# A four-layer graph network on one core: the four sums of a step added up in PSUM by block before DVE takes them over

## The reference, cut to what matters

```python
h = jnp.maximum(_layernorm(x, axis=-1), 0.0)     # before each layer
# layer 0: segment_sum(h[src] * weight, dst), product with W, batch norm, relu
# layer 1
messages = jax.nn.relu(x @ W_msg.T + b_msg)
aggregated = jax.ops.segment_sum(messages[src], dst, num_segments=x.shape[0])
# layer 2
msg_in = jnp.concatenate([h[src], h[dst], e], axis=-1)
messages = jax.nn.silu(msg_in @ w1 + b1) @ w2 + b2
messages = messages * jax.nn.sigmoid(msg_in @ wg + bg)
agg = segment_sum(messages, dst) / jnp.maximum(segment_sum(ones, dst), 1.0)[:, None]
# layer 3: 256 message values for each edge
mid_s0 = w0 * se * es
mid_s1 = w3 * jnp.einsum('eui,ei->eu', ve, ev) / SQRT3
mid_v0 = (w1 * se)[:, :, None] * ev[:, None, :]
mid_v1 = (w2 * es)[:, :, None] * ve
ns, nv = segment_sum(mid_scal, dst) / 4, segment_sum(mid_vec, dst) / 4
```

## Time and profile before

| | |
|---|---|
| median of three runs | 5316.91 us (5315.05 to 5318.62) |
| the profiled execution | 5316.99 us, its span 5315.3 us |
| busy: PE | 4052.6 us (76%) |
| busy: DVE | 3452.5 us (65%) |
| busy: ACT | 1883.2 us (35%) |
| busy: POOL | 3748.9 us (71%) |

### The profile page before, as it was taken

The page is one execution under the profiler, slowest core; times in us unless marked ns, Lnnn a source line. Parts: engine busy times, 40 slices in busy tenths (PEclk is TensorE's granted clock), DMA queues, the critical chain, the costliest instruction groups (busy, mean ns, idle before and its releaser), DMA issues. The chain is left out here.

```text
span 5315.3 us, 109575 instructions
## 1 busy us (share of the span) xinstructions
PE 4052.6 (76%) x21313; PEld 3103.9 (58%) x21314; DVE 3452.5 (65%) x11120; ACT 1883.2 (35%) x5384; POOL 3748.9 (71%) x3284
## 2 busy tenths in 40 slices
PE   2888888888884466666667899999998678787787
PEld 2666666666663244444445677777777555555556
DVE  6655565655553633333335788888887688888886
ACT  2322222222221122222222444333433555555553
POOL 1788888888885377777773477777776277777772
PEclk9555555555555778888788999999999888888889
DMA  5665665566666266666663566666665233233232
GB/s 171 104 90 88 93 89 93 89 93 89 93 89 119 67 180 178 181 180 179 180 179 102 159 202 198 198 196 197 195 198 159 79 57 56 56 56 57 56 56 58
DMA packets 936530, 658.88 MB, mean 124 GB/s; under 512 B 402828, under 2 KB 878955, under 8 KB 934290
## 3 DMA queue, kind: packets, MB, share of 16 engines
q0 software_dynamic: 211152, 281.46, 26.3%
q1 hardware_dynamic: 722294, 372.22, 26.2%
q10 hardware_dynamic: 2812, 2.00, 0.1%
HBM read 462.32 MB, written 224.57 MB: 129 GB/s over the span
## 5 line engine op out<-in xcount | busy, mean ns | idle before, releaser
L726 POOL DMA_INDIRECT sums<-work,idx x832 | 1288.2, 1548 | 323.4 <-issue 176.7
L1495 DVE TENSOR_TENSOR x_and_big<-psum,x_and_big 128x129 f32 (+2 forms) x2496 | 823.9, 330 | 709.7 <-PE psum L842 489.9
L758 POOL DMA_INDIRECT G<-table,src_it x832 | 861.0, 1035 | 322.9 <-issue 253.2
L758 POOL DMA_INDIRECT G<-table,work x782 | 770.5, 985 | 269.6 <-issue 236.5
L758 POOL DMA_INDIRECT x_and_big<-table,work x782 | 762.5, 975 | 273.4 <-issue 236.8
L895 PE MATMUL psum<-work 128*128 128x128 f32 x1664 | 627.5, 479 | 193.6 <-DVE work L1542 169.8
L1142 ACT ACTIVATE work<-psum,work 128x128 f32<-128x128 f32 x832 | 305.8, 368 | 1069.7 <-PE psum L887 1066.2
L895 PEld LDWEIGHTS psum<-work 128*128 128x128 f32 x1664 | 412.6, 307 | 381.4 <-DVE work L1542 378.1
L842 PE MATMUL psum<-x_and_big,oh 128*128 x1664 | 332.1, 361 | 365.1 <-DMA x_and_big<-table,work 251.7
L989 PE MATMUL psum<-x_and_big,oh 128*128 x1664 | 508.4, 459 | 130.3 <-DVE x_and_big L1682 119.7
L887 PE MATMUL psum<-x_and_big,work 128*128 x1664 | 589.5, 457 | 0.0
(11 more groups left out here) (240 smaller groups left out, 7285.8 us busy)
## 6 DMA issues: line engine op xcount, KB each, us to landing
work<-e_pre SPq DMA_DIRECT2D x832, 128.0 KB
e_pre<-work SPq DMA_DIRECT2D x196, 512.0 KB
G<-e_meta SPq DMA_DIRECT2D x832, 64.0 KB
work<-e_a SPq DMA_DIRECT2D x195, 128.0 KB
e_a<-in_edge_attr_dram SPq DMA_DIRECT2D x51, 488.0 KB
sums<-work,idx POOLq DMA_INDIRECT x832
G<-table,src_it POOLq DMA_INDIRECT x832
sums<-x_and_big POOLq DMA_DIRECT2D x4, 3264.0 KB
```

The costliest lines, as they stand in the source:

```text
L726: pool.indirect_dma_start(sums[k % COPIES], bass.IndirectOffsetOnAxis(ap=idx[:, k:k + 1], axis=0), z_out[:, k, :], None, compute_op=ALU.ad ...
L758: pool.indirect_dma_start(to, None, tab, bass.IndirectOffsetOnAxis(ap=of[:, n:n + 1], axis=0)).then_inc(quad_in[n // 4 % AHEAD], 16)
L1495: v.tensor_tensor(to, ps, to, ALU.add).then_inc(EDGE[layer]["acc_done"], 1)
```

## The change

The four products of a step now go to one window in PSUM that has four slots, one for each of four consecutive blocks from the block of the step's first item on. Items with the same block add up in the same slot. For that

- the prologue computes `slot_row`, for each item its block less that of its step's first item (0 to 3), and takes at least one item for each block, so that four consecutive items never reach over more than four blocks. `blk_row`, `row_row` and `slot_row` become partitions 0, 32 and 64 of one tensor, `item_rows`;
- PE loads 16 slot numbers beside the 16 row or block numbers every fourth step, and the place of products two to four comes from a register;
- before the four products PE sets the window to zero by products of a row of zeros with ones, both bf16: two of 128x2x129 in layer 1, one of 128x512 in layer 2, two of 128x512 in layer 3. The four products then add to what is there (`start=False`);
- DVE adds the whole window to four consecutive blocks of `acc[layer]` with one instruction (`add_window`; 128x516, 128x512 and 128x1024), at the place where the first of the four adds stood;
- `acc` has three more blocks in each layer. In layer 3 they are taken from the room of x: six more blocks of x go to `x_keep` and back (34 of 50, 28 before), and the cleared areas grow from 6450, 6400 and 12800 to 6837, 6784 and 13568 elements a partition.

```diff
-KEEP = (NBT * (D + L3W) - RING3 * L3W) // D
+KEEP = (NBT * D + (NBT - 3) * L3W - RING3 * L3W) // D
...
+            def window(win, j, reg):
+
+                return win[:, 0, :] if j == 0 else at(win, pe.snap(reg, min_val=0, max_val=3))
+
+            def zero_bank(to):
+
+                t.matmul(to, zeros_b[0:1, :], ones_b[0:1, 0:1].unsqueeze(2).broadcast_to([1, to.shape[1], to.shape[2]]), start=True, stop=True)
...
                 def top(item):
                     pe.load(regs, row_row[0:1, bass.ds(item + (LEAD - 4), RING)])
+                    pe.load(slots, slot_row[0:1, bass.ds(item + (LEAD - 4), RING)])
...
-                            pe.wait_ge(ph["acc_done"], 4 * q - 8)
+                            pe.wait_ge(ph["acc_done"], q - 2)
                         pe.wait_ge(ph["oh_ready"], q)
+                        for lo in (0, 2):
+                            t.matmul(win1[o][:, lo:lo + 2, :], zeros_b[0:1, :],
+                                     ones_b[0:1, 0:1].unsqueeze(2).broadcast_to([1, 2, wid]), start=True, stop=True)
                         for j in range(4):
                             slot = pe.snap(regs[k % 4 * 4 + j], min_val=0, max_val=ROWS - 1) % RING1
-                            mm = t.matmul(bank[2 * o + j // 2][:, j % 2 * wid:(j % 2 + 1) * wid], oh[:, (k - 1) % 4 * 4 + j, :],
-                                          at(G1, slot), start=True, stop=True)
+                            mm = t.matmul(window(win1[o], j, slots[k % 4 * 4 + j]), oh[:, (k - 1) % 4 * 4 + j, :],
+                                          at(G1, slot), start=False, stop=True, skip_group_check=True)
...
                         if item(8):
-                            pe.wait_ge(ph["acc_done"], 4 * q - 28)
+                            pe.wait_ge(ph["acc_done"], q - 7)
+                        zero_bank(win2[(k - 6) % 2])
                         pe.wait_ge(ph["msg_done"], q - 5)
...
+                        for h in (0, 2):
+                            zero_bank(win3[k % 2][:, h:h + 2, :])
...
+            link(v.tensor_scalar(D_[:, 0:NB], D_[:, 0:NB], 1.0, None, ALU.max))
...
-            def add_item(layer, reg, ps, before):
+            def add_window(layer, reg, win, landed_quads, before):
 
                 b = dve.snap(reg, min_val=0, max_val=NB)
-                to = at(acc[layer], b)
+                to = acc[layer][:, bass.ds(b, 4), :]
+                dve.wait_ge(EDGE[layer]["agg_done"], landed_quads)
                 if before is not None:
                     dve.wait_ge(EDGE[layer]["acc_done"], before)
-                v.tensor_tensor(to, ps, to, ALU.add).then_inc(EDGE[layer]["acc_done"], 1)
+                v.tensor_tensor(to, win, to, ALU.add).then_inc(EDGE[layer]["acc_done"], 1)
```

76 lines of the change are left out of this document (32 added, 44 removed).

## The result

The changed kernel takes 5335.3 us (median of five runs, 5333.2 to 5343.7) against 5316.9 (5313.1 to 5318.6) of the kernel before on the same chip: a ratio of 1.0041, 95% interval 1.003 to 1.0052. It is 18 us slower; 5309.5 was forecast, with "within 0.2%" as the likeliest case. The profiled execution, one of the longer of the five, has a span of 5341.4 us, 26.1 more than that of before. On another chip the same kernel took 5338.3 against 5310.2 (1.0044, interval 1.003 to 1.0058).

What follows compares the result with a forecast made beforehand. POOL's train of gathers, plus a draining tail, was taken to bound each layer. The terms −5.5 − 5 + 1 + 2.1 + 0 = −7.4 us gave 5309.5 against the median of 5316.91; range 5288 to 5340.

Steps and rivals of the forecast that it cites:

- Rival (b): Slower by PE in layer 2: its step becomes 5.6 us, over 5.35, costing +52 us, time 5362; chance 12%.
- Part 1: DVE's 2496 adds (823.9 us) become 624 sums (539 us): 285 us less busy time, nothing on the path.
- Part 2: PE's zeros and addresses: +0.3 to 0.9 us a step, hidden; layer 2's step 5.08, at most 5.3, under 5.35.
- Part 3: Layer 1 after its last gather: 13 PE groups at 2.0 us each, −5.5 us, between −0.3 and −12.
- Part 4: Layer 3 after its last gather: 13 steps of 2.45 us, −5 us; at half clock a loss up to 18.
- Part 5: The end of layer 2, its last three steps and final adds: +1 us, from −1 to +3.
- Part 6: What is cleared and copied: +2.1 us, of which clearings 1.3 and the prologue 0.8.
- Part 7: Gathers lengthened by DVE instructions with both operands in SBUF: 0, ±15 us; −3 in layer 2, +3 in layer 3.
- rival (c): Slower by gathers: layer 3's two-SBUF instructions catch one every step, +17 up to +35, 5327 to 5345 us; chance 13%.

Runs made afterwards that it cites:

- e_before_turn48: The kernel before with PE's and DVE's layer 2 loops 48 steps long instead of 24: 5314.2 us, ratio 1.0004.
- a_l2_old: The changed kernel with layer 2 put back to four places and four adds a step, no zeros or second register load there: 5309.8 us, ratio 1.000.
- c_l2_turn48: The changed kernel with PE's and DVE's layer 2 loops 48 steps long instead of 24: 5309.0 us, ratio 0.9993.
- k_l3_one_sum: The changed kernel with layer 2 put back and PE's layer 3 as before, DVE keeping one sum there (output wrong): 5287.3 us, ratio 0.9959.
- h_l2_one_sum: The changed kernel with PE's layer 2 as before, DVE keeping one sum a step there (output wrong): 5319.7 us, ratio 1.0015.
- r_dve_zero12: The changed kernel with DVE instead of PE zeroing the windows in layers 1 and 2, from the third window on: 5368.8 us, ratio 1.0113.

## Why the prediction was wrong

**The bound: right for before, wrong for after.** POOL's train of gathers bounded all three layers before, and e_before_turn48 confirms it for layer 2. Rival (b), given 12%, is what happened, with +28 us in place of its +52.

**Part 1, DVE: right.** 543 us of sums against 539. They bought nothing by themselves.

**Part 2, PE in layer 2: the step that failed.** I put PE's step at 4.48 + 0.32 + 0.28 = 5.08, at most 5.3, against 5.35, and called it hidden. The terms in the trace: the zeros 0.31; 0.1 more for the four products, with their addresses from registers, and 0.1 more ahead of the zeros, where I took 0 (at most 0.21), so the step is 4.99; the second register load 1.1 us at every fourth step, 0.28 a step, as bounded. The first load was hidden before (4.5 us a step, see above), the second isn't: the steps with two are 6.07 to 6.19. Both loads got longer, too, and not by the tensor of three partitions they come from: in a_l2_old PE makes one load from it at a time.

```profile
L922 PEldq TENSOR_LOAD <-item_rows x53: 1109/1280/1295, 2976.0 to 4114.4; - x53
...
L922 PEldq TENSOR_LOAD <-item_rows x53: 1103/1109/1270, 2977.8 to 4091.5; - x53
```

The first row is the changed kernel, with a second load right behind each, the second row a_l2_old. Between two turns the mean is thus (3 × 4.99 + 6.12) / 4 = 5.27, within my 5.3 and under POOL's 5.35.

What the sum lacked was in the profile before: the stop at the turn of the loop. I had taken the step from between two turns, at its shortest, and called it PE's step. With the turn, 24 steps need 18 × 4.99 + 5 × 6.12 + 12.4 = 132.8 us, 5.53 a step, over POOL's 128.4 and 5.35; before it was some 112.9. The 19.9 us between are 12.2 for zeros and addresses, 5.6 for the second loads and 2.0 at the turn. c_l2_turn48 shows the term by itself: half the turns gave 22 of the 28 us back.

**Part 3, tail of layer 1: −5.5 forecast, −1.3 and −1.9 measured** in the two profiles of the changed kernel. Steps of 1.4 (full clock) and 2.6 us (half) are there as bounded, but two of them have the two loads and the wait for DVE's sum in their way: 3.49 and 3.57 us from L860 to L860 (2863.46 to 2867.03), the second with the last sum behind it.

```profile
2862.05 1.16 PE L860 MATMUL psum<-x_and_big,oh 128*128 x8
...
2863.46 1.16 PE L860 MATMUL psum<-x_and_big,oh 128*128 x8
...
2866.59 0.51 PE L856 MATMUL psum<-ones_b,zeros_b 1*128 1x258 bf16 x2 [1.96 <-DVE x_and_big L1523]
...
2869.27 0.70 DVE L1523 TENSOR_TENSOR x_and_big<-psum,x_and_big 128x516 f32 x1 [3.62 <-PE psum L860]
```

**Part 4, tail of layer 3: −5 forecast, +9.9 and −3.6 measured.** The step of 2.45 us is right (2.46, 3.1 to 3.2 with loads), and in the second profile, in which the last message product starts only 4.3 us after the last gather, the tail is nearly as forecast. What I did not price is how late PE and DVE can be when the last gather lands, 14.9 us in the first profile: I took the half clock as a matter of the tail alone. In mid-stage PE at half clock needs 7.3 us a step. The claim that PE's 967 of 1057 us are "hidden" was read from a mean; 930 us busy were measured, and the mean was under the window all the same. My price at half clock was too low as well: eight passes take 3.78 us there and the two zeros 0.96, some 4.7 a group, and over 13 groups that would be a loss of 24 us by an estimate from these rows, not 18. k_l3_one_sum, without PE's additions, has a tail 14 us shorter than before.

**Part 5, tail of layer 2: +1 forecast, +14.0 and +14.9 measured.** With PE as the bound it enters the tail with the ring full: at the start of the last gather nine groups of sum products were still to come, before six. This is part 2's error again; a_l2_old has −1.8.

**Part 6: right in size.** The clearing went from 10.76 to 11.40 us (0.65 forecast):

```profile
4204.34 11.40 POOL L750 MEMSET x_and_big<- 128x13568 f32 x1
```

Between the layers it is 2.9 and 2.5 us more where 0.33 and 0.65 were counted; what makes the other 4 is not known. In the prologue, 5.6 and 7.9 us are lost in the two profiles of the changed kernel, not 0.8. ACT issued two loads of the edge weights in 3.7 us before (first row) and in 15.1 after (second row), and its counting of blocks began late:

```profile
6.97 3.74 ACTq L1067 DMA_DIRECT2D e_meta<-in_edge_weight_dram  x2
...
7.27 15.05 ACTq L1090 DMA_DIRECT2D e_meta<-in_edge_weight_dram  x2
```

The thirteen other kernels with the same prologue lost 0 to 2.3 us, although the issue lasted 8 to 14.3 us in them. What makes it long, and why only the changed kernel itself loses more, was not tried and stays open.

**Part 7, stretched gathers: the rule right in the main, the amounts not.** Forecast −3 in layer 2 and +3 in layer 3. By the busy times, layer 1 went from 24 to 13 us, layer 2 from 76 to 58, layer 3 from 32 to 21. In all kernels with layer 3 changed and PE's zeros there it is 19 to 25, against 30 to 32 with the four adds: the five two-SBUF instructions in one row collide less, not more. Layer 1's 13 us is not typical of the change: its second profile has 17, the other kernels with that layer changed 18 to 26. In layer 2 the 18 us had no value, as POOL waited anyway. That a stretched gather "then ends with" the instruction was read wrong: it ends 0.82 us after it, in the earlier trace rows (2204.91 and 2205.73) as in all kernels here (0.81 to 0.82 for nine of ten). The rule of the Trainium skill (SBUF — State Buffer, "SBUF: two separate sides") is borne out once more by 1.96 us beside L1641, and h_l2_one_sum and r_dve_zero12 show what it can cost: a phase that holds took 16 and 33 us more of layer 2 than before.

**The sum.** −7.4 was forecast and +26.1 came, in the profiled execution. Layer 2 makes 28 of the difference of 33.5 and the prologue 5. That the range of 5288 to 5340 had the median in it is luck: it was made wide for rival (c), which didn't happen, and left out (b), which did but cost less than its 52 us. The sign was wrong, and 12% for (b) was too little with a margin of 0.3 us on a step that had been measured at its best.

## What to carry to other kernels

The time of a step that an engine needs is its time over a whole turn of the loop, with the register loads and the stop at the branch, not the shortest step between two turns; compare that with the bound before work is moved to it. Work moved from an engine that idles to one that is close behind the bound buys nothing and can cost, and near the bound the steps at half clock (7.3 us here against a bound of 5.0) count, not the mean. Unused turns of a loop are free until such a shift makes them the price: 22 us in layer 2 for half the turns.
